# Audio tower on one core: gates of the power attention by a broadcast load, expert outputs added by DMA, a second attention in groups of three tiles, and its causal mask written into PSUM by TensorE

## The chip, the core and the metric

The kernel runs on one core of one Trainium2 chip. The metric is the device time of one launch in microseconds (us). Each engine (PE is the matrix engine, DVE the vector engine, ACT the scalar engine, POOL GpSimd, SP the engine that issues most loads) works through a queue of its own in order, and semaphores tie the queues together. The matrix engine has two clock levels, 1.2 and 2.4 GHz; the profile gives the granted clock as a share of full speed.

## The reference

64 sequences of 23 patches give 1472 tokens of 512 features. Five parts follow one another, each added to the running state h:

```python
h = tok(x)                      # layer norm, x @ W + b, layer norm
h = h + power_attention(ln(h))  # 8 heads, 2 query groups each, width 128
h = h + moe(ln(h))              # 16 experts, 4 per token, and a shared one
h = h + attention(ln(h))        # 16 query heads, 4 key heads, width 32
h = h + bitlinear_ffn(ln(h))    # ternary weights, width 2048
```

Of these, three places are touched.

```python
logG = jnp.cumsum(log_g, axis=1)                 # power attention
gate = logG[:, :, :, None] - logG[:, :, None, :]
a = jnp.where(causal, qk ** 2 * jnp.exp(gate), 0.0)
...
acc + cw[:, None] * _swiglu_ffn(x, wg, wu, wd)   # sum over a token's experts
...
scores = jnp.where(causal[None, None], scores, -jnp.inf)   # attention
A = jax.nn.softmax(scores, axis=-1)
```

## The kernel before

The tokens lie in 12 tiles of 128 rows, or, where whole sequences matter, in 16 blocks of 92 tokens (4 sequences), of which 4 make a chunk of 368 columns. fp32 products are made of three fp16 matmuls (high by high, low by high, high by low; L852 to L854), and a "low" part is made by `split_lo` on DVE (L1295).

**Power attention.** A hardware loop over 8 heads, in it 4 chunks. Per chunk PE projects q, k and v from the transposed state (`nT_hi`, `nT_lo`) with the unit's weights `wa_hi`, `wa_lo`, makes scores (L950), multiplies by v (L967), turns the result `yn` (L983) and applies the output weights. DVE accumulates the outputs (L1432). The decay gate of a chunk wants, in each of 92 rows, the cumulative logs of all 368 columns. They are made by an fp32 matmul of `ones` by `Dg` (L935), where `Dg` is the log gates spread over a triangle by DVE (L1447); ACT copies the result out of PSUM (`gt`, L635), and DVE subtracts the row's own sum and adds the mask. At the last chunk of a head the next head's weights are made: ACT writes `wa_hi` (L550) and DVE `wa_lo` (L1295, `unit_a_lo`), next to pieces of the experts' weights `we_sp` (`expert_hi`, `expert_lo`) that are prepared during the heads. Ahead of the loop stand the gate's logits, their logs `lg`, and one cumulative matmul by the triangle `tri` (L904).

**Experts.** 61 routed tiles leave weighted outputs `yt` in a table in DRAM, `yslot`. Then, on POOL's queue, `collect(k)` issues four indirect gathers per tile k of 128 tokens (L484, 48 in all) into a ring of three tiles' buffers, and DVE adds the four rows of `wide` to h (`returned`, L1698 to L1701). For the layer norm ahead of the second attention DVE makes sums, POOL the inverse square root of the variance (`root`, L446; eight tiles, then four), and ACT normalises (L560). ACT copies the turned tile into fp16 (L565), DVE makes the low part.

**Second attention.** The work is in 4 chunks c of 16 sequences. `project(c, j)` makes five blocks of q and k and one of v on PE; per block DVE shuffles halves (L1743), POOL multiplies by cosine and sine (L516, L517) and DVE adds (L1753, L1754). `scores(c)` is 64 fp32 matmuls of 32 x 23 (L1177, 128 recorded) into four banks of PSUM. `centred(c)` on DVE adds the mask (L1761, 128 x 1472), takes the maximum (L1764) and subtracts it (L1765); ACT takes the exponent; `weights(c)` sums (L1771) and divides (L1777); PE turns the weights (`turn`, L1186) and multiplies by V (`weighted`, L1199); ACT and DVE make high and low parts of the result (`y_high`, `y_low`, L1784). The order is written out by hand, in each engine's own function: PE does scores(c), all projections of c+1, turn(c), weighted(c). At the end the output weights and the ternary feed-forward follow.

## Time and profile before

| | us |
|---|---|
| three runs | 1563.63, 1563.95, 1555.3 |
| median | 1563.63 |
| profiled execution, its own time | 1547.85 |
| its span | 1545.9 |

| stage, us from the span's start | |
|---|---|
| tokens to state, layer norms | 0 to 145 |
| eight heads of the power attention | 151 to 700 |
| routing | 715 to 800 |
| experts, 61 routed tiles and the shared one | 800 to 1145 |
| gathers of the expert outputs | 1124.3 to 1196 |
| second attention | 1196.5 to 1340.6 |
| its output weights, then the feed-forward | 1340.6 to the end |

Over the whole span PE is busy 85%, DVE 61%, ACT 42%, POOL 18%. A share over the span mixes stages with different limits, so the profile is read stage by stage: first which engine is busy there, then what the others wait for.

### The profile page before, as it was taken

What the parts mean: (1) busy time and instruction counts of PE and PEld (TensorE: products, weight loads), DVE (VectorE), ACT (ScalarE), POOL (GpSimd) and SP (SyncE); (2) the same over time, 40 slices, a digit from 0 to 9 for tenths busy, and PEclk for the clock granted to TensorE, in tenths of its full rate; (3) what the DMA queues carried; (4) which work ended last, traced back from release to release, by engine and by line L of the source; (5) the groups of instructions that cost most, each with busy time, mean ns of one, the idle gap of its engine ahead of it and who ended that gap; (6) DMA issues with size and microseconds to landing.
All of it is one profiled execution on the core that took longest, in us unless ns stands there. A gap on an engine that the chain in (4) does not pass through costs nothing.

```text
span 1545.9 us, 30851 instructions
## 1 busy us (share of the span) xinstructions
PE 1316.9 (85%) x10735; PEld 837.6 (54%) x10736; DVE 937.2 (61%) x1940; ACT 644.0 (42%) x1098; POOL 283.0 (18%) x342
## 2 busy tenths in 40 slices
PE   6887999999999999996759999999950788668997
PEld 3445767677776777774424444444520566424443
DVE  5775456556665555658663555554376455588886
ACT  3445434444444444542314444444420433126664
POOL 2443000000000000000012233233276334020000
PEclk9986999999999999996779999999985778689999
DMA  5222142423334342421315767874265000000000
GB/s 177 69 102 69 56 170 116 163 109 135 133 132 170 136 163 82 163 83 75 132 62 181 258 240 256 283 241 162 91 193 168 2 2 3 1 1 8 21 20 31
DMA packets 40254, 179.87 MB, mean 116 GB/s; under 512 B 8512, under 2 KB 9024, under 8 KB 32384
## 3 DMA queue, kind: packets, MB, share of 16 engines
q0 software_dynamic: 18208, 95.41, 17.4%
q1 hardware_dynamic: 18528, 71.03, 13.0%
q10 hardware_dynamic: 3456, 12.58, 2.4%
q8 instruction: 41, 0.67, 0.2%
q14 instruction: 21, 0.17, 0.0%
HBM read 131.32 MB, written 47.69 MB: 116 GB/s over the span
## 4 chain that ended last, share of the span: by engine, by line
PE 56%; DVE 18%; issue 13%; POOL 6%; ACT 5%; DVEq 1%; DMA 1%; ACTq 0%; POOLq 0%; SPq 0%
PE ps L852 14%; PE ps L853 13%; PE ps L854 13%; POOL wide L484 3%; PE ps L967 3%; PE ps L950 3%; PE ps L1177 2%; DVE ff L1870 2%; DVE amf L1877 1%; PE ps L935 1%; PE ps L983 1%; DVE wa_lo L1295 1%; POOL rt_out L446 1%; PE ps L1046 1%; PE ps L1248 1%
## 5 line engine op out<-in xcount | busy, mean ns | idle before, releaser
L852 PE MATMUL ps<-nT_hi,wa_hi 128*128 128x368 f16 x448 | 146.4, 327 | 15.9 <-DVE wa_lo L1295 15.9
L853 PE MATMUL ps<-nT_lo,wa_hi 128*128 128x368 f16 x448 | 146.0, 326 | 0.0
L854 PE MATMUL ps<-nT_hi,wa_lo 128*128 128x368 f16 x448 | 145.6, 325 | 0.0
L476 POOL DMA_INDIRECT xg<-xrow,idx x61 | 61.1, 1001 | 277.1 <-PE ps L1046 101.7
L1629 DVE SCALAR_TENSOR_TENSOR nrm<-ps,xg,nrm 128x256 f32<-128x256 f32 x61 | 29.5, 484 | 133.5 <-ACT nrm L694 107.6
L852 PE MATMUL ps<-wa_hi,nT_hi 128*92 128x128 f16 (+1 forms) x560 | 108.8, 238 | 0.0
L853 PE MATMUL ps<-wa_lo,nT_hi 128*92 128x128 f16 (+1 forms) x560 | 107.6, 236 | 0.0
L854 PE MATMUL ps<-wa_hi,nT_lo 128*92 128x128 f16 (+1 forms) x560 | 107.6, 236 | 0.0
L852 PE MATMUL ps<-wide,xT 128*128 x244 | 93.4, 383 | 12.3 <-issue 6.3
L663 ACT ACTIVATE yT_hi<-ps 128x368 f16<-128x368 f32 x64 | 27.2, 474 | 164.0 <-PE ps L983 164.0
L471 POOL DMA_DIRECT2D wsp<-we_sp x16 | 8.6, 537 | 468.7 <-DVE we_sp L1295 468.7
L1432 DVE SCALAR_TENSOR_TENSOR wide<-ps,wide 128x368 f32<-128x368 f32 x128 | 69.1, 540 | 41.0 <-PE ps L854 41.0
L853 PE MATMUL ps<-wide,xT 128*128 x244 | 93.2, 382 | 0.0
L854 PE MATMUL ps<-wide,xT 128*128 x244 | 93.0, 381 | 0.0
L1248 PE MATMUL ps<-qw,qT 128*128 128x512 bf16 x384 | 89.1, 387 | 2.7 <-DVE ff L1870 2.6
L852 PE MATMUL ps<-yT_hi,wb_hi 128*128 128x368 f16 x256 | 82.6, 323 | 1.2 <-DVE yT_lo L1479 1.2
L853 PE MATMUL ps<-yT_lo,wb_hi 128*128 128x368 f16 x256 | 82.6, 323 | 0.0
L854 PE MATMUL ps<-yT_hi,wb_lo 128*128 128x368 f16 x256 | 82.6, 323 | 0.0
L622 ACT ACTIVATE qk<-ps 128x368 f32<-128x368 f32 x96 | 45.2, 478 | 89.1 <-PE ps L854 89.0
L1457 DVE TENSOR_TENSOR a<-sq,E 92x368 f32<-92x368 f32 x64 | 31.7, 534 | 82.3 <-ACT sq L651 82.3
L852 PEld LDWEIGHTS ps<-wa_hi,nT_hi 128*92 128x92 f16 (+1 forms) x560 | 67.4, 120 | 22.3 <-ACT qk L622 17.2
L685 ACT ACTIVATE xT<-ps 128x1024 f16<-128x1024 f16 x61 | 62.3, 1024 | 28.9 <-PE ps L1046 21.2
(307 smaller groups left out, 3403.9 us busy)
## 6 DMA issues: line engine op xcount, KB each, us to landing
we_st<-in_we POOLq DMA_DIRECT2D x16, 1536.0 KB, 6.9
wsp<-we_sp POOLq DMA_DIRECT2D x16, 1536.0 KB, 5.4
wide<-wsp SPq DMA_DIRECT2D x16, 1536.0 KB, 7.4
yslot<-yt POOLq DMA_DIRECT2D x61, 256.0 KB, 4.3
wq_st<-in_ffq SPq DMA_DIRECT2D x24, 512.0 KB, 4.5
wq_st<-in_ffq ACTq DMA_DIRECT2D x24, 512.0 KB, 3.9
wide<-in_wa SPq DMA_DIRECT2D x10, 1024.0 KB, 4.8
xt<-in_x SPq DMA_DIRECT2D x12, 512.0 KB, 3.5
```

The lines of the kernel that those rows point to most:

```text
L476: pool.indirect_dma_start(Q["xg"][:, g % 4, :].bitcast(U32), None, xrow, bass.IndirectOffsetOnAxis(ap=idx[:, g:g + 1], axis=0)).then_inc(x ...
L484: pool.indirect_dma_start(h1[:, 4 * (k % 3) + j, :], None, yslot, bass.IndirectOffsetOnAxis(ap=slot[:, k, j:j + 1], axis=0)).then_inc(xg_i ...
L622: nc.scalar.activation(B["qk"][:, j, :], ps[:, (5 * c + j) % 2, 0:CW], ACT.Copy, scale=1.0 / WS).then_inc(b_ev, 1)
L685: nc.scalar.activation(Q["xT"][:, p].rearrange("p a b -> p (a b)"), ps[:, p, :].bitcast(F16), ACT.Copy).then_inc(m_xe, 1)
L852: nc.tensor.matmul(dst, lhs[0], rhs[0], start=start, stop=False)
L853: nc.tensor.matmul(dst, lhs[0], rhs[1], start=False, stop=False)
L854: return nc.tensor.matmul(dst, lhs[1], rhs[0], start=False, stop=stop)
L950: ins = nc.tensor.matmul(ps[0:AT, 2 + j, a * REP * AT:(a + 1) * REP * AT], B["qk"][:, 2, tok], B["qk"][:, 0:2, tok], start=True, stop=True)
L967: ins = nc.tensor.matmul(ps[0:AT, 4 + 2 * j + a, r * (DH + 1):(r + 1) * (DH + 1)], B["a"][0:AT, j, a, r, :], B["v1"][0:AT, 2 * j + a, :], ...
L1248: ins = nc.tensor.matmul(ps[:, 2 * (f % 2) + q, :], Gm["qT"][:, b, ds(k * P, P)], qw[:, q, b * FF + f * 512:b * FF + (f + 1) * 512], start ...
L1432: V.scalar_tensor_tensor(acc, ps[:, 6 + blk % 2, 0:CW], 1.0 / (WS * AS), acc, ALU.mult, ALU.add).then_inc(b_acc, 1)
L1457: V.tensor_tensor(B["a"][0:AT, j], B["sq"][0:AT, j], B["E"][0:AT, 2 * j:2 * j + 2].unsqueeze(2).broadcast_to([AT, 2, REP, AT]), ALU.mult). ...
```

## The change

Four things are done.

1. The gates' cumulative logs for the columns no longer come from a matmul per chunk. One more matmul ahead of the heads gives them transposed (128 rows: 16 blocks by 8 heads); they are copied to SBUF, stored to DRAM (`lgd`), and once per head a broadcast load on SP's queue writes the head's row of 1472 values into 92 partitions (`gr`). The first of DVE's two passes reads `gr` instead of ACT's copy. The gate's logits move to another bank of PSUM, and two projections of the first head stand ahead of the cumulative matmuls. `unit_a_hi` and `unit_a_lo` are issued ahead of `expert_hi` and `expert_lo(., 0)` at a head's last chunk.
2. The gathers add into h themselves. `share(k, j)` waits until the transfer before it to the same tile has landed. DVE's adds are gone. The tiles come in four groups of three, with layer norm and root per group, and the gathers of the later groups stand between POOL's cosines.
3. The second attention's order is written anew: `turn(c - 1)` and `weighted(c - 1)` are done during chunk c, layer-norm tiles of the next group lie between projections, and most of the multiplications by the sine go from POOL to DVE.
4. The mask is written into PSUM by a bf16 matmul of identity by mask per bank (4 per chunk) ahead of the scores, which then accumulate on it; DVE's mask pass is gone, and its maximum and its subtraction read PSUM.

The diff, cut to its core:

```diff
+            sp.wait_ge(g_lg, 2)
+            sp.dma_start(lgd.rearrange("h (a p) -> (h a) p", p=AT), B["lgt"][:, :]).then_inc(init_out, 16)
+            sp.wait_ge(init_out, 32)
+            sp.dma_start(B["gr"][0:AT], lgd[0:1, :].broadcast_to([AT, T])).then_inc(gr_in, 16)
...
+                sp.wait_ge(b_gr, i + 1)
+                sp.dma_start(B["gr"][0:AT], lgd[ds(i + 1, 1), :].broadcast_to([AT, T])).then_inc(gr_in, 16)
...
-            def collect(k):
-                for j in range(TOPK):
-                    pool.indirect_dma_start(h1[:, 4 * (k % 3) + j, :], None, yslot,
-                                            bass.IndirectOffsetOnAxis(ap=slot[:, k, j:j + 1], axis=0)).then_inc(xg_in[k % 3], 16)
-
-            pool.wait_ge(zero_out, 16)
+            def share(k, j):
+
+                if j or k >= 6:
+                    pool.wait_ge(sh_in[k % 6], SHARES[k % 6] + 64 * (k // 6) + 16 * j)
+                pool.indirect_dma_start(h[:, k, :], None, yslot, bass.IndirectOffsetOnAxis(ap=slot[:, k, j:j + 1], axis=0),
+                                        compute_op=ALU.add).then_inc(sh_in[k % 6], 16)
+
+            def shares(g, j):
+                for k in range(GT * g, GT * g + GT):
+                    share(k, j)
...
-            for k in range(NT):
-                if k >= 3:
-                    pool.wait_ge(c_h, ready(NT + k - 3))
-                collect(k)
-
-            for n, x in enumerate((slice(0, EARLY), slice(EARLY, NT))):
-                root(rc_ask, 2 + n, rt_in[:, x], rt_out[:, x], rc_done)
+
+            def turned_root(g):
+                x = slice(GT * g, GT * g + GT)
+                root(rc_ask, 2 + g, rt_in[:, x], rt_out[:, x], rc_done)
...
+                if c and j < 4:
+                    nc.gpsimd.tensor_tensor(Fm["qs"][:, j, :], Fm["qs"][:, j, :], sinT[:], ALU.mult).then_inc(f_cos, 1)
+
+            for j in range(TOPK):
+                shares(0, j)
+                shares(1, j)
+            pool.wait_ge(m_y, VT)
+            shares(2, 0)
+            turned_root(0)
+            nc.gpsimd.memset(Fm["qp"][:, :, :, SL:], 0.0).then_inc(f_pad, 1)
+            shares(3, 0)
+            turned_root(1)
+            cosine(0, 0)
+            shares(2, 1)
+            cosine(0, 1)
+            cosine(0, 2)
+            shares(2, 2)
+            cosine(0, 3)
+            cosine(0, 4)
+            shares(2, 3)
+            pool.wait_ge(wa_lo, UNITS + 1)
+            nc.gpsimd.memset(st_a[:], 0.0).then_inc(f_pad, 1)
+            shares(3, 1)
+            for j in range(5):
+                cosine(1, j)
+            shares(3, 2)
+            turned_root(2)
+            shares(3, 3)
+            turned_root(3)
+            for c in range(2, CH):
...
-                    pe.wait_ge(b_ev, free(5 * g + 3))
-                    pe.wait_ge(b_D, g + 1)
-                    nc.tensor.matmul(ps[0:AT, (5 * c + 3) % 2, 0:CW], ones[0:AT, 0:AT], B["Dg"][0:AT].rearrange("p a b -> p (a b)"),
-                                     start=True, stop=True).then_inc(b_pj, 1)
...
+            pe.wait_ge(g_lg, 1)
+            nc.tensor.matmul(ps[0:AT, 7, 0:16 * HEADS], tri[0:AT, :], B["lg"][0:AT].rearrange("p a b -> p (a b)"),
+                             start=True, stop=True)
+            nc.tensor.matmul(ps[:, 6, 0:AT], B["lg"][0:AT].rearrange("p a b -> p (a b)"), tri[0:AT, :],
+                             start=True, stop=True).then_inc(g_cum, 1)
...
+                for g in range(G4):
+                    nc.tensor.matmul(ps[:, 2 + g, 0:CW], identb[:], maskb[:], start=True, stop=False)
                 for s in range(16):
                     for g in range(G4):
                         d = slice(HD * g, HD * (g + 1))
                         ins = nc.tensor.matmul(ps[:, 2 + g, s * SL:(s + 1) * SL], Fm["qp"][d, s].rearrange("p j t -> p (j t)"),
-                                               Fm["kr"][d, s * SL:(s + 1) * SL], start=True, stop=True)
+                                               Fm["kr"][d, s * SL:(s + 1) * SL], start=False, stop=s == 15)
...
+                if c + 1 < CH:
+                    pe.wait_ge(f_sb, c + 2)
+                else:
+                    pe.wait_ge(f_lo, 4 * c)
...
+            def row_turn_l1(k):
+                ln_turn(2 * NT + k, k % 2, k % 2)
+
+            for k in range(GT):
+                row_turn_l1(k)
+            pe.wait_ge(wa_lo, UNITS)
             pe.wait_ge(wb_lo, UNITS)
-            for j in range(3, 6):
-                project(0, j)
+            project(0, 0)
+            project(0, 1)
             for c in range(CH):
+                k = GT * (c + 1)
+                for j in range(2, 6):
+                    project(c, j)
+                    if c % 2 == 0 and j < 5:
+                        row_turn_l1(k + j - 2)
+                if c:
+                    turn(c - 1)
+                if c == 0:
+                    project(c + 1, 0)
+                    project(c + 1, 1)
                 scores(c)
-                if c + 1 < CH:
-                    for j in range(6):
-                        project(c + 1, j)
-                turn(c)
-                weighted(c)
+                if c == 1:
+                    weighted(c - 1)
+                    for j in range(GT):
+                        row_turn_l1(k + j)
+                if 0 < c < CH - 1:
+                    project(c + 1, 0)
+                    project(c + 1, 1)
+                if c > 1:
+                    weighted(c - 1)
+            turn(CH - 1)
+            weighted(CH - 1)
...
-                    V.tensor_tensor(B["Dg"][0:AT], B["lgh"][0:AT, 4 * c:4 * c + 4].unsqueeze(2).broadcast_to([AT, 4, AT]),
-                                    tri[0:AT].unsqueeze(1).broadcast_to([AT, 4, AT]), ALU.mult).then_inc(b_D, 1)
-                    dve.wait_ge(b_ev, ready(5 * g + 3))
-                    order(V.tensor_tensor(B["gt"][0:AT], B["gt"][0:AT],
+                    if c == 0:
+                        dve.wait_ge(gr_in, 16 * (i + 1))
+                        dve.sem_inc(passed, 1)
+                    order(V.tensor_tensor(B["gt"][0:AT], B["gr"][0:AT, c * CW:(c + 1) * CW].rearrange("p (a t) -> p a t", a=4),
...
+                    if c == CH - 1:
+                        unit_a_lo(i + 1)
                     if c % 2:
                         expert_lo(2 * i + c // 2, 0)
-                    if c == CH - 1:
-                        unit_a_lo(i + 1)
...
-            def returned(k):
-                dve.wait_ge(xg_in[k % 3], SLOTS_IN[k % 3] + 64 * (k // 3 + 1))
-                dve.sem_inc(passed, 1)
-                y = [h1[:, 4 * (k % 3) + j, :] for j in range(TOPK)]
-                V.tensor_tensor(y[0], y[0], y[1], ALU.add)
-                order(V.tensor_tensor(y[2], y[2], y[3], ALU.add))
-                order(V.tensor_tensor(row(k), row(k), y[0], ALU.add))
-                V.tensor_tensor(row(k), row(k), y[2], ALU.add).then_inc(c_h, 1)
...
-                order(V.tensor_tensor(S.rearrange("p (g h) s -> p g h s", g=G4),
-                                      ps[:, 2:6, 0:CW].rearrange("p g (h s) -> p g h s", s=SL),
-                                      mask1[:].unsqueeze(1).unsqueeze(1).broadcast_to([P, G4, 16, SL]), ALU.add))
-                order(V.tensor_reduce(Fm["mx"][:], S, AX.X, ALU.max))
-                V.tensor_tensor(S, S, Fm["mx"][:].unsqueeze(2).broadcast_to([P, 64, SL]), ALU.subtract).then_inc(f_sb, 1)
+                src = ps[:, 2:6, 0:CW].rearrange("p g (h s) -> p g h s", s=SL)
+                mx = Fm["mx"][:].rearrange("p (g h) -> p g h", g=G4)
+                order(V.tensor_reduce(mx, src, AX.X, ALU.max))
+                V.tensor_tensor(S.rearrange("p (g h) s -> p g h s", g=G4), src, mx.unsqueeze(3).broadcast_to([P, G4, 16, SL]),
+                                ALU.subtract).then_inc(f_sb, 1)
...
+            def low(k):
+                ln_low(2 * NT + k, k, k % 2)
+
+            for k in range(GT):
+                low(k)
+            group_shift(1)
             for c in range(CH):
+                k = GT * (c + 1)
+                rotate(c, 0)
+                rotate(c, 1)
+                if c:
+                    weights(c - 1)
+                for j in range(2, 5):
+                    if c % 2 == 0:
+                        low(k + j - 2)
+                    rotate(c, j)
+                rotated(c)
+                if c == 0:
+                    dve.wait_ge(wa_hi, UNITS + 1)
+                    split_lo(wo[1][:].rearrange("p a b -> p (a b)"), st_a[:], wo[0][:].rearrange("p a b -> p (a b)"), wa_lo)
+                if c == 1:
+                    group_stats(2)
+                    group_shift(2)
                 centred(c)
-                if c + 1 < CH:
-                    for j in range(2):
-                        rotate(c + 1, j)
-                weights(c)
-                if c + 1 < CH:
-                    for j in range(2, 5):
-                        rotate(c + 1, j)
-                    rotated(c + 1)
-                y_low(c)
+                if c:
+                    y_low(c - 1)
+                if c == 1:
+                    for j in range(GT):
+                        low(k + j)
+                    group_stats(3)
+                    group_shift(3)
+            weights(CH - 1)
+            y_low(CH - 1)
```

How rows move on three engines. First POOL before the change, from the last keeps of expert outputs (`yslot<-yt`) over the gathers to the first cosines; `rt_out` is the inverse square root, `qraw` and `qs` are a projected block and its shuffled copy.

```order
L480 DMA yslot<-yt 128x512 x6
L484 DMA wide<-yslot,slot 128x512 x48
L446 TENSOR_TENSOR rt_out<-rt_in,neg_half 128x8
L446 TENSOR_TENSOR rt_out<-rt_in,neg_half 128x4
L516 TENSOR_TENSOR qraw<-qraw,cosT 128x368
L517 TENSOR_TENSOR qs<-qs,sinT 128x368
```

The same place after the change.

```order
L501 DMA yslot<-yt 128x512 x6
L507 DMA h<-yslot,slot 128x512 x27
L467 TENSOR_TENSOR rt_out<-rt_in,neg_half 128x3
L550 MEMSET qp 128x64x9
L507 DMA h<-yslot,slot 128x512 x3
L467 TENSOR_TENSOR rt_out<-rt_in,neg_half 128x3
L540 TENSOR_TENSOR qraw<-qraw,cosT 128x368
L507 DMA h<-yslot,slot 128x512 x3
L540 TENSOR_TENSOR qraw<-qraw,cosT 128x368 x2
L507 DMA h<-yslot,slot 128x512 x3
L540 TENSOR_TENSOR qraw<-qraw,cosT 128x368 x2
L507 DMA h<-yslot,slot 128x512 x3
```

Of the gathers 27 now stand ahead of the first root, and 21 more come later, in groups of three between roots, fills and cosines.

DVE at the last chunk of a head, before: the accumulation of the outputs, then the two splits, then the normalising factor `rn` of `yn`.

```order
L1432 SCALAR_TENSOR_TENSOR wide<-ps,wide 128x368
L1437 REGISTER_ALU
L1295 SCALAR_TENSOR_TENSOR we_sp<-we_st,we_sp 128x1024
L1298 REGISTER_ALU
L1295 SCALAR_TENSOR_TENSOR wa_lo<-wide,wa_hi 128x2048
L1471 TENSOR_SCALAR rn<-ps 92x4
```

And after.

```order
L1538 SCALAR_TENSOR_TENSOR wide<-ps,wide 128x368
L1403 REGISTER_ALU
L1400 SCALAR_TENSOR_TENSOR wa_lo<-wide,wa_hi 128x2048
L1543 REGISTER_ALU
L1400 SCALAR_TENSOR_TENSOR we_sp<-we_st,we_sp 128x1024
L1578 TENSOR_SCALAR rn<-ps 92x4
```

The split of `wa_lo` now stands ahead of that of `we_sp`; what follows both is as it was.

PE in the second attention, before: V's projection, turn, weighting, the next chunk's scores, its next projections.

```order
L1161 MATMUL ps<-wb_lo,nT_hi 32x128 x4
L1161 MATMUL ps<-wb_hi,nT_lo 32x128 x4
L1186 MATMUL ps<-ident,wide 128x128 x16
L1199 MATMUL ps<-wide,V 32x92 x64
L1177 MATMUL ps<-kr,qp 128x23 x64
L852 MATMUL ps<-nT_hi,wa_hi 128x368
L853 MATMUL ps<-nT_lo,wa_hi 128x368
```

And after, at the chunk c = 1.

```order
L1238 MATMUL ps<-wb_hi,nT_lo 32x128 x4
L1270 MATMUL ps<-ident,wide 128x128 x16
L1256 MATMUL ps<-maskb,identb 128x368 x4
L1260 MATMUL ps<-kr,qp 128x23 x64
L1287 MATMUL ps<-wide,V 32x92 x64
L925 MATMUL ps<-ident,nrm 128x128 x12
L930 MATMUL ps<-nT_hi,wa_hi 128x368
L931 MATMUL ps<-nT_lo,wa_hi 128x368
```

The turn of the chunk before is now ahead of the scores, the weighting behind them, and three tiles of layer norm are turned (`nrm`, L925) before the next projection; the four mask matmuls are the row ahead of the scores.

## Rows read from the trace of the kernel before

The engines' columns of the first group are PE, PEld, DVE, ACT and POOL in this order.

**Rows 1.** Busy time: us, engines' busy time (instructions), PE clock, DMA share, GB/s.

```profile
287.30:355.70 68.40, 66.12 (x570) 49.79 (x569) 40.55 (x80) 30.00 (x51) 2.15 (x4) 1.00 0.37 138
...
1145.00:1196.00 51.00, 0.03 (x1) 0.00 (x0) 35.54 (x60) 1.18 (x2) 37.29 (x33) 0.53 0.65 194
```

**Rows 2.** Timeline, ACT: start, us, engine, line, operation, [idle before <-releaser].

```profile
1196.52 1.52 ACT L560 ACTIVATE nrm<-h,nb,rt_out 128x512 f32<-128x512 f32 x2 [50.34 <-DVE nb L1327]
```

**Rows 3.** Timeline, PE in the second attention.

```profile
1228.94 7.04 PE L1177 MATMUL ps<-kr,qp 32*128 32x23 f32 x128 [6.87 <-DVE qp L1754]
...
1259.54 7.04 PE L1177 MATMUL ps<-kr,qp 32*128 32x23 f32 x128 [3.82 <-DVE nT_lo L1784]
...
1317.19 7.04 PE L1177 MATMUL ps<-kr,qp 32*128 32x23 f32 x128 [3.80 <-DVE nT_lo L1784]
...
1338.73 1.83 PE L1199 MATMUL ps<-wide,V 32*32 32x92 f32 x128
```

**Rows 4.** Groups of instructions: form, count, busy us, mean ns, idle before.

```profile
L935 PE MATMUL ps<-Dg,ones 92*92 92x368 f32 x64 | 25.7, 483 | 0.0
```

**Rows 5.** Timeline, PE around one gate matmul in a head.

```profile
272.85 0.32 PE L854 MATMUL ps<-nT_hi,wa_lo 128*128 128x368 f16 x1
273.01 0.78 PE L935 MATMUL ps<-Dg,ones 92*92 92x368 f32 x2
273.74 0.26 PE L852 MATMUL ps<-wa_hi,nT_hi 128*92 128x128 f16 x1
```

**Rows 6.** DMA issues: tile<-source, queue, count, KB each, median us to landing.

```profile
wide<-in_wb SPq DMA_DIRECT2D x10, 512.0 KB, 3.5
...
tb<-in_tb SPq DMA_DIRECT2D x1, 256.0 KB, 9.2
```

**Rows 7.** Timeline, PE in the first head.

```profile
151.30 0.73 PE L904 MATMUL ps<-lg,tri 92*92 92x128 f32 x2 [6.13 <-DVE lg L1418]
...
165.52 1.93 PE L967 MATMUL ps<-v,a 92*92 92x129 f32 x16
```

**Rows 8.** Timeline, PE at the boundary of two heads.

```profile
285.68 0.33 PE L852 MATMUL ps<-nT_hi,wa_hi 128*128 128x368 f16 x1 [2.28 <-DVE wa_lo L1295]
...
287.56 0.80 PE L983 MATMUL ps<-ident,yn 92*128 92x92 f32 x8
```

**Rows 9.** Timeline, DVE at the same boundary.

```profile
282.13 1.22 DVE L1295 SCALAR_TENSOR_TENSOR we_sp<-we_st,we_sp 128x1024 f16<-128x1024 f32 x1
283.26 2.29 DVE L1295 SCALAR_TENSOR_TENSOR wa_lo<-wide,wa_hi 128x2048 f16<-128x2048 f32 x1
...
286.85 0.69 DVE L1473 TENSOR_TENSOR yn<-ps,rn 92x512 f32<-92x512 f32 x1
```

**Rows 10.** Timeline, POOL: the first, third and last of 48 gathers.

```profile
1124.34 1.00 POOL L484 DMA_INDIRECT wide<-yslot,slot  x1 [2.02 <-DMA yslot<-yt]
...
1126.93 0.95 POOL L484 DMA_INDIRECT wide<-yslot,slot  x1 [0.30 <-issue]
...
1189.23 1.02 POOL L484 DMA_INDIRECT wide<-yslot,slot  x1 [0.30 <-issue]
```

**Rows 11.** Instructions of the line of the gathers: their landing times.

```profile
DMA to landing us min/median/max: 3.3/3.7/7.3
```

**Rows 12.** Timeline, DVE: the softmax of chunk 0.

```profile
1236.05 1.69 DVE L1761 TENSOR_TENSOR wide<-ps,mask 128x1472 f32<-128x1472 f32 x1 [7.16 <-PE ps L1177]
...
1239.50 1.69 DVE L1765 TENSOR_TENSOR wide<-wide,mx 128x1472 f32<-128x1472 f32 x1
...
1245.25 1.69 DVE L1771 TENSOR_REDUCE rd<-wide 128x64 f32<-128x1472 f32 x1 [1.99 <-ACT wide L747]
...
1247.56 1.69 DVE L1777 TENSOR_TENSOR wide<-wide,rd 128x1472 f32<-128x1472 f32 x1
```

**Rows 13.** Groups of instructions: POOL's multiplication by the cosine.

```profile
L516 POOL TENSOR_TENSOR qraw<-qraw,cosT 128x368 f32<-128x368 f32 x20 | 19.4, 968 | 71.8 <-DVE qs L1743 71.8
```

**Rows 14.** Busy time, PE alone, scores(0): us, busy, clock, DMA share, GB/s.

```profile
1228.90:1236.00 7.10, 7.05 (x129) 0.50 0.01 2
```

More of the change, by code:

```diff
@@ L390, in _ @@
                 unit_b(i + 1)
+                sp.wait_ge(b_gr, i + 1)
+                sp.dma_start(B["gr"][0:AT], lgd[ds(i + 1, 1), :].broadcast_to([AT, T])).then_inc(gr_in, 16)
+            sp.wait_ge(q_abs, 3 * HEADS - 2)
+            for m in range(3):
+                sp.dma_start(wq_st[:, m, :], t["ffq"][m, HEADS - 1]).then_inc(q_in, 16)
+            sp.wait_ge(wa_lo, HEADS)
+            unit_a(HEADS)
+            sp.wait_ge(wb_lo, HEADS)
+            unit_b(HEADS)
             for k in range(NT):
@@ L771, in _, with normed @@
[L771 to L784 removed]
+            def normed(k):
+                if k % GT == 0:
+                    act.wait_ge(ln_sh, 3 + k // GT)
+                ln_norm(2, k, k % 2)
@@ new lines, in high @@
+            def high(k):
+                ln_high(2 * NT + k, k, k % 2)
+            normed(0)
+            normed(1)
+            high(0)
+            normed(2)
+            high(1)
+            high(2)
+            moved(0, 0)
+            moved(0, 1)
+            for c in range(CH):
+                k = GT * (c + 1)
+                if c % 2 == 0:
+                    normed(k)
+                    normed(k + 1)
+                moved(c, 2)
+                if c % 2 == 0:
+                    high(k)
+                    normed(k + 2)
+                moved(c, 3)
+                if c % 2 == 0:
+                    high(k + 1)
+                moved(c, 4)
+                if c % 2 == 0:
+                    high(k + 2)
+                moved(c, 5)
+                if c == 0:
+                    act.wait_ge(wa_in, 16 * (UNITS + 1))
+                    nc.scalar.activation(wo[0][:].rearrange("p a b -> p (a b)"), st_a[:], ACT.Copy, scale=WS).then_inc(wa_hi, 1)
+                else:
+                    weights_turned(c - 1)
+                if c == 1:
+                    normed(k)
+                    normed(k + 1)
+                    exponential(c)
+                    y_high(c - 1)
+                    high(k)
+                    normed(k + 2)
+                    high(k + 1)
+                    high(k + 2)
+                    moved(c + 1, 0)
+                    moved(c + 1, 1)
+                else:
+                    if c + 1 < CH:
+                        moved(c + 1, 0)
+                        moved(c + 1, 1)
+                    exponential(c)
+                    if c:
+                        y_high(c - 1)
@@ L786, in f_square @@
+            weights_turned(CH - 1)
+            y_high(CH - 1)
             def f_square(k, p, half):
@@ L1236, in q_turn @@
                 ins.then_inc(w_tr, 1)
-            pipeline(pe, NT, [(0, out_rows)])
+            for k in range(NT):
+                out_rows(k, k % 2, k // 2)
             def gate_up(k, fs):
@@ L1421, in _ @@
             dve.wait_ge(g_cum, 1)
+            V.tensor_copy(B["lgt"][:], ps[:, 6, 0:AT]).then_inc(g_lg, 1)
             order(V.tensor_copy(B["LG"][0:AT].rearrange("p a b -> p (a b)"), ps[0:AT, 7, 0:128]))
```

157 lines of the change are left out of this document (64 added, 93 removed).

## The prediction

> **What bounds the kernel.** I read, in this order, busy time by stretch, the costliest lines, the timelines of the places that the diff touches, and the landing times of transfers. In the steady heads PE is the limit: of the 68.40 us of one head it is busy 66.12, at full clock, while DVE has 40.55 and ACT 30.00 [rows 1]. What leaves PE there leaves the end; what leaves DVE or ACT does not. Before the second attention it is the reverse: from 1145 to 1196 us PE does nothing, and POOL is busy 37.29 of 51.00 with issuing the gathers of the expert outputs [rows 1]. ACT idles 50.34 us and begins the second attention at 1196.52 [rows 2]. That stage runs to 1340.56, 144.0 us, and no engine bounds it: the rows show PE waiting for the rotated operands, for the weights, for the low half of V's operand [rows 3]. It is a chain of hand-overs.
>
> **Heads: the gate matmul.** Each of 32 chunks (8 heads, 4 chunks) had one fp32 matmul of ones by Dg, recorded in two halves, 64 of 0.483 us [rows 4]. What counts is its slot: the row before it starts at 272.85 and gives way after 0.16 (the pace of its neighbours), the row after starts at 273.74 [rows 5], so 0.73 us. 32 x 0.73 = **-23.4 us**, all on the path. Its ACT eviction and the DVE product go too, at nothing, since both engines wait for PE. In its place stand one small matmul ahead of the heads and one broadcast load per head, 529 KB, on SP's queue. Chunk 0 of a head waits for it; it is issued when the head before has read its last quarter. The nearest row is a 512 KB load, 3.5 us [rows 6]; the slowest near it is 9.2 us for 256 KB, at the start. A head's first gate is wanted about ten us after its first matmul, and DMA was at 0.37 of its capacity in a head [rows 1], so loads 2 to 8 hide.
>
> **First head.** PE idled 6.13 us ahead of the cumulative matmul, for DVE's logs [rows 7]. Two projections now stand ahead of it and fill that idle time. The first AV came at 165.52; its gates now need lgt, a store, the load of 3.5 us and the passes behind it, and I get about 161.5: 4.0 us, 0.7 of which is the first Dg slot already counted, so **-3.3** (bounds -4.7, load hidden, and +1, load at 9.2). The load has 92 rows on both sides. The Trainium skill, page "DMA: Bandwidth & Descriptors", section "Why a DMA increments its semaphore by 16 and not by 1", says that a transfer uses the largest number of engines up to 16 that divides both outer sizes: 4 here. By its 27 GiB/s an engine the load lands, as an estimate, after 6.7 us and the sum gives 3.2 us less; no row of this profile shows a load of 92 partitions.
>
> **Boundary of heads.** PE waits 2.28 us for wa_lo [rows 8], seven times. DVE splits an expert's weights first (1.22 us), then wa_lo, then makes yn [rows 9]. The change swaps the two, so wa_lo lands 1.2 us sooner. But PE's matmul L983 wants yn, whose last piece is made from 286.85 to 287.54, and L983 starts at 287.56 [rows 8, 9]: the same DVE passes stand ahead of yn in either order. The wait is renamed from wa_lo to yn; I take 0.25 each, **-1.7** (bounds 0 and -8.5, where all 1.2 us come through). Heads together: -28.4.
>
> **Start of the second attention.** POOL issued 48 gathers, from 1124.34 to 1189.23: 1.38 us each [rows 10]. Then came the root of eight tiles, and ACT at 1196.52. Now the groups are of three tiles, and 27 issues stand ahead of the first root: 1124.34 + 27 x 1.38 = 1161.6; root and shift 1.4; ACT starts at 1163.0, **-33.5**. The four DVE adds per tile that followed the landings are gone: the transfer adds. Each tile takes four of them in a row, and POOL waits for one to land before it issues the next to that tile. A round over six tiles is 6 x 1.38 = 8.3 us, over the longest landing of a plain gather, 7.3 (median 3.7) [rows 11], so at plain prices the wait costs nothing. The accumulating form is nowhere in this profile. Bounds: bare pace 1.25 an issue (0.95 and 0.30 [rows 10]) gives -37; every landing at twice the maximum, 14.6 us a round, puts the last round at 1124.3 + 43.8 = 1168, its landings at up to 1185 and the start at 1188, -8.5. Bus time of a plain gather: 0.65 of 51 us at 194 GB/s, 256 KB each, is 37.7 gathers, 0.88 us each [rows 1]; twice that, 1.76, is above the pace of 1.38: the last share of the first group, 21st in line, lands at 1124.3 + 37 + 3.7 = 1165, and the start is about 3 later, -30.5. The Trainium skill, page "Collectives: The Full Stack", section "The bandwidth ceiling: the fold count and why AG ≠ RS ≠ AR", says just that: an adding transfer reads two sources and runs at half the rate. By it the sum gives 3 us less; no row here shows it.
>
> **Length of the second attention.** The 21 other gathers, 29 us of POOL, now lie within it, between cosines. I went through the new order leg by leg. (a) Start to scores(0): 32.4 before (1228.94 - 1196.52), now 26: three tiles' layer norm instead of eight, but 9 gathers between the cosines (range 22 to 32.4). (b) scores(0) to scores(1): 23.6 before (1259.54 - 1235.98), now 19: centring 3.4 (two passes of 1.69; the mask pass is gone, and its row shows that reading PSUM costs no more), exponent about 4.1 (from 1241.19 to 1245.25, where its sum starts), weights 4.0 (1245.25 to 1249.25) [rows 12], five cosines of 0.97 [rows 13], rotation 2.2. (c) scores(1) to scores(2), all on PE or waited for by it: centring 3.4, weighting 1.8, y_high 1.6, three layer-norm tiles 4 and their turns 2, six projections 14.3 (72 matmuls at 0.2, between 0.16 at full clock [rows 5] and twice that), turn 3, hence 30. (d) scores(2) to scores(3): the same without layer norm, turns and y_high, 22.5. (e) Four score blocks, 4 x (7.04 + 0.62) = 30.6; the 0.62 is four mask matmuls of 368 columns, 0.16 us apart at full clock like the head's [rows 5]. (f) Tail: 16.3 before (1340.56 less 1317.19 + 7.04 [rows 3]), now 16.6: one DVE pass of 1.7 less, y(2) ahead of the last weights 2.3 more. Sum 144.7 against 144.0, +1. The mask by itself is thus worth -1.7 x 4 + 0.6 x 4 = -4. Clock: scores(0) came after 6.87 us of idle PE and ran at a granted 0.50, so at 1.2 GHz [rows 3, 14]. Now scores(0) and scores(2) follow busy PE; I take -4 (between 0, no change, and -14, all four at the full 2.4 GHz: half of 28). Stage net **-3** (range -14 to +10: leg (a) +6.4, the others +4).
>
> **Sum.** -28.4 - 33.5 - 3.0 = -64.9. The profiled execution took 1547.85 (span 1545.9), which gives 1483. It stood 15.8 under the median of its runs, 1563.63, with one run at 1555.3. Against the median: **1499 us**. Under 1% of 1563.63, 15.6 us, this kernel can hardly be told from no change.
>
> **The rivals.**
> - *Landings set the pace* (chance 0.15). POOL waits in every round; the share of bus time, 0.65 already [rows 1], speaks for it, the 8.3 us round against 3.7 speaks against. At 14.6 a round, 25 us of the gain are gone: 1524.
> - *The queues of the new second attention collide* (0.12). PE, DVE and POOL are in order, and weights(c-1) now stands between the rotations of c; a late gather in POOL holds the cosines, these the scores. At 6 us for each of legs (a) to (d) less overlap, 20 are lost: 1519.
> - *Clock stays high* (0.15). PE is fed through all four score blocks, -10 more than I take: 1489. Against it, PE idle before scores, 6.87 and 3.8 us [rows 3], is not all filled.
> - *Slower than before* (0.03). The adding gather is bound by its own rate. The gain of the heads, 28.4, stays, so ACT would have to start 31.4 us later than 1196.5, and the tail of gathers for later groups end past the cosines: from 3.7 us a gather ((1302 - 1124.3)/48), four times the 0.88 of bus time, the kernel is slower. For it: only that nothing here shows the form.
> - *My sum* has 0.55. The -23.4 of the gate matmul is as safe as a row can make it, which is why the signs hardly mix.
>
> The range: the low end is the forecast with the high clock and the whole boundary wait (-10, -6.8) and something of the first head, 1476 to 1479, and 3 for the runs' spread; the high end is the first rival and 8 more. I take 1474 to 1533. Faster by over 1%: all but the slow rival and half of a stack of the first two, 0.93; within 1% 0.04; slower 0.03.
>
> **What would show it.** In the changed profile: a head of about 65.2 us (68.40 less 4 x 0.73 and 0.25) with PE busy for 63, no matmul on Dg, and no wait for the broadcast load after the first head; PE's wait at a boundary still near 2 us, but now for yn; ACT's first row of the second layer norm at 1196.5 - 28.4 - 33.5, about 1135; gathers issued 1.38 apart with no wait for a landing; the stage from there about 141 us; two DVE passes of 1.7 instead of three between scores and exponent; granted clock over 0.5 in scores(0). A round of gathers over 10 us, a wait of POOL for landings, or scores 25 us apart in leg (b) would make the sum wrong, and a head of still over 67.5 us would refute the first step.

## The result, and the profile after

The changed kernel took 1511.69 us (median of 4 runs, 1510.18 to 1513.29) against 1560.72 of the kernel before: a ratio of 0.9689 (95% interval 0.9655 to 0.9724), 49 us less. When both were measured again, on one chip, they took 1509.55 and 1551.43, 0.9743 (0.9720 to 0.9767), 42 us less. The forecast was 1499, 65 us less; the direction and the range (1474 to 1533) held, the size was a third too large. The two profiled executions differ by less still: spans 1545.9 and 1510.1, so 35.8. The kernel before has a wide spread: its 27 runs lie between 1547.0 and 1564.0, and its profiled one, 1547.85, is among its fastest. The changed kernel's 9 lie between 1508.9 and 1513.6. Why, is read from experiment e5 below; the account of steps goes by the two traces.

First, busy time of a head, in the columns of [rows 1].

```profile
284.23:349.38 65.15, 63.58 (x560) 48.94 (x561) 38.21 (x75) 28.22 (x47) 2.16 (x4) 1.00 0.41 153
```

A head takes 65.15 instead of 68.40, PE is busy 63.58 of it: the period held to 0.1 us and PE's busy time to 0.6 (65.2 and 63 were forecast). The timeline of PE, first head, first boundary, and then the scores of the second attention, to the first matmul of its output weights ([rows 7], [rows 8] and [rows 3] are the same places before).

```profile
167.20 3.72 PE L1037 MATMUL ps<-v,a 92*92 92x129 f32 x16 [5.36 <-DVE a L1564]
...
219.07 0.33 PE L930 MATMUL ps<-nT_hi,wa_hi 128*128 128x368 f16 x1 [1.11 <-DVE wa_lo L1400]
222.11 0.54 PE L1053 MATMUL ps<-ident,yn 92*128 92x92 f32 x4 [0.46 <-DVE yn L1580]
...
1187.09 0.80 PE L1256 MATMUL ps<-maskb,identb 128*128 128x368 bf16 x4 [2.51 <-DVE qp L1851]
1187.81 7.03 PE L1260 MATMUL ps<-kr,qp 32*128 32x23 f32 x128
...
1212.86 1.41 PE L1256 MATMUL ps<-maskb,identb 128*128 128x368 bf16 x4 [5.18 <-DVE qp L1851]
1214.19 7.04 PE L1260 MATMUL ps<-kr,qp 32*128 32x23 f32 x128
...
1252.21 3.77 PE L1260 MATMUL ps<-kr,qp 32*128 32x23 f32 x128
...
1278.56 1.41 PE L1256 MATMUL ps<-maskb,identb 128*128 128x368 bf16 x4 [3.60 <-DVE qp L1851]
1279.89 7.04 PE L1260 MATMUL ps<-kr,qp 32*128 32x23 f32 x128
...
1304.94 0.39 PE L930 MATMUL ps<-wo_hi,nT_hi 128*128 128x512 f16 x1
```

The boundary's wait is split, 1.11 for wa_lo and 0.46 for yn. The first AV product (the gated scores `a` by v) starts at 167.20, later than before (165.52), after 5.36 us of idle PE, and takes 3.72 instead of 1.93. Why it is late, DVE's timeline says: the first row that reads the broadcast load.

```profile
164.47 0.54 DVE L1555 TENSOR_TENSOR gt<-gr,LGh 92x368 f32<-92x368 f32 x1 [10.06 <-DMA gr<-lgd]
```

SP issued that load at 155.27, so it took 9.2 us. DVE waited for no other of the eight loads. Now POOL: first, second and 27th gather, and the first root ([rows 10]).

```profile
1103.99 1.66 POOL L507 DMA_INDIRECT h<-yslot,slot  x1 [2.02 <-DMA yslot<-yt]
1105.96 1.57 POOL L507 DMA_INDIRECT h<-yslot,slot  x1 [0.30 <-issue]
...
1154.49 1.55 POOL L507 DMA_INDIRECT h<-yslot,slot  x1 [0.31 <-issue]
1155.48 1.47 POOL L467 TENSOR_TENSOR rt_out<-rt_in,neg_half 128x3 f32<-128x3 f32 x1
```

An adding gather holds POOL for 1.55 us where a plain one held it for 0.95, and the next starts 1.85 later (1.94 on average, 50.50 / 26, with two that took longer). No wait of POOL for a landing costs time: one of the 48 gathers is released by a landing, and it starts after the same 0.31 as its neighbours. ACT begins the second attention at 1157.19 ([rows 2]):

```profile
1157.19 1.52 ACT L607 ACTIVATE nrm<-h,nb,rt_out 128x512 f32<-128x512 f32 x2 [32.19 <-DVE nb L1432]
```

| step | forecast | in the traces |
|---|---|---|
| up to the first gather (1124.34 to 1103.99) | -28.4 | -20.4 |
| first gather to ACT's start (72.18 to 53.20) | -33.5 | -19.0 |
| length of the second attention (144.0 to 147.7) | -3 | +3.7 |
| behind it | 0 | -0.2 |
| sum | -64.9 | -35.8 |

### The profile page after: what moved, and what is told of

It reads as the page before. It is cut to its first block, busy times and chain, and to the rows that moved or that the text cites. A ratio compares the mean times of both kernels' runs of the same rounds, so it can differ in the third digit from the quotient of the medians.

```text
span 1510.1 us, 30384 instructions
## 1 busy us (share of the span) xinstructions
PE 1302.2 (86%) x10676; PEld 833.5 (55%) x10690; DVE 889.8 (59%) x1862; ACT 630.0 (42%) x1066; POOL 308.1 (20%) x336
## 4 chain that ended last, share of the span: by engine, by line
PE 55%; DVE 18%; issue 13%; POOL 6%; ACT 4%; DMA 2%; DVEq 1%; ACTq 0%; POOLq 0%; SPq 0%
PE ps L930 13%; PE ps L932 13%; PE ps L931 13%; POOL h L507 3%; PE ps L1037 3%; PE ps L1020 3%; PE ps L1260 2%; DVE ff L1980 2%; DVE amf L1987 1%; PE ps L1353 1%; PE ps L1053 1%; POOL rt_out L467 1%; PE ps L1121 1%; PE ps L1371 1%; DMA xg<-xrow,idx 1%
## 5 line engine op out<-in xcount | busy, mean ns | idle before, releaser
L930 PE MATMUL ps<-nT_hi,wa_hi 128*128 128x368 f16 x448 | 147.7, 330 | 11.9 <-DVE wa_lo L1400 8.1
L507 POOL DMA_INDIRECT h<-yslot,slot x48 | 79.7, 1661 | 15.4 <-issue 13.1
```

The source lines that it names most:

```text
L507: pool.indirect_dma_start(h[:, k, :], None, yslot, bass.IndirectOffsetOnAxis(ap=slot[:, k, j:j + 1], axis=0), compute_op=ALU.add).then_inc ...
L930: nc.tensor.matmul(dst, lhs[0], rhs[0], start=start, stop=False)
```

## The experiments

All are edits of the changed kernel. They ran on three chips, each beside runs of the kernel before, whose medians there were 1556.9 (e1, e2, e4, e6), 1552.0 (e3, e5, e7, e8) and 1551.4 (e9 and the last three). A total that is 1 or 2 us off that of the changed kernel (1511.7, again 1509.6) therefore settles nothing by itself; the traces do.

Terms: a "leg" is the time from one block of scores to the next, or from ACT's start to the first, or from the last to the output weights; the "tail" is that last leg; the "stage" is the whole second attention, from ACT's start to the first matmul of the output weights.

**e2 and e3: why the first broadcast load took 9.2 us.**

```diff
# e2, likewise at the load in the loop
-            sp.dma_start(B["gr"][0:AT], lgd[0:1, :].broadcast_to([AT, T])).then_inc(gr_in, 16)
+            sp.dma_start(B["gr"][0:96], lgd[0:1, :].broadcast_to([96, T])).then_inc(gr_in, 16)
# e3
             sp.dma_start(B["gr"][0:AT], lgd[0:1, :].broadcast_to([AT, T])).then_inc(gr_in, 16)
+            sp.wait_ge(gr_in, 16)
```

> The changed kernel with the broadcast load of the gate's row written to 96 partitions instead of 92. In the changed kernel the first of these loads took 9.2 us, and the first AV product of head 0 stood idle 5.36 us for it, starting at 167.20. Theory A, 92 rows are spread over few DMA engines (the Trainium skill, DMA: Bandwidth & Descriptors, Why a DMA increments its semaphore by 16 and not by 1: 4 for 92, 16 for 96): it lands after 3 to 4.5 us, the product starts at about 162 to 163, total 4 to 6 us less, 1506 to 1508. Theory B, it is slowed by the other loads then in flight (feed-forward weights, head weights, the expert weights): landing stays near 9 us, total 1512.

> The changed kernel, but SP issues nothing behind the first broadcast load of the gate's row until it has landed, so that three 512 KB feed-forward loads and the head's weights don't run beside it. Theory A, few DMA engines for 92 rows set its 9.2 us: it lands only 0 to 2 us sooner, total 1510 to 1512. Theory B, the loads beside it set it: it lands after 4 to 5 us, first AV product at 162 to 163, total 1506 to 1508.

e2: 1504.19. The load is issued at 155.12 and used at 159.33, 4.2 us, though it moves more bytes beside the same neighbours. e3: 1508.04; issued at 154.75, used at 161.49, 6.7 us with nothing beside it. How many engines carried it can be read from the DMA share while it ran alone:

```profile
156.00:161.00 5.00, 4.44 (x44) 3.42 (x41) 0.00 (x0) 0.59 (x1) 0.00 (x0) 1.00 0.26 102
```

The last two columns are DMA share and GB/s: 0.26 of 16 engines is 4.2, about the 4 of theory A in e2. The AV product of e2 on PE's timeline, and PE's clock in the 5 us from it (us, busy, clock, DMA share, GB/s):

```profile
162.06 1.97 PE L1037 MATMUL ps<-v,a 92*92 92x129 f32 x16 [1.18 <-DVE a L1564]
```

```profile
162.06:167.06 5.00, 5.00 (x41) 1.00 0.92 374
```

The same window of the changed kernel:

```profile
167.20:172.20 5.00, 5.00 (x21) 0.50 0.43 158
```

So theory A of e2 holds (few engines for 92 rows), with a share for the neighbours: of 9.2 us, 5.0 go with four more rows, 2.5 with the neighbours gone (between the two theories of e3). The estimate worked out in the prediction from the Trainium skill (DMA: Bandwidth & Descriptors, Why a DMA increments its semaphore by 16 and not by 1), 6.7 us for 4 engines, is what e3 measured; 4.7 of it are 541,696 bytes over four engines, and where its other 2.0 come from it does not say. The rest of the gain is the clock: after 5.36 us of idle PE the granted clock was 0.50, 1.2 GHz, for these 5 us; after 1.18 it was 1.00. From the start of AV to the first boundary it is 51.87 us in the changed kernel and 48.49 in e2, so e2's first boundary comes 8.5 sooner: 5.1 by AV's start, 3.4 by the clock. Its first gather, at 1096.78, is 7.2 sooner; the stretch from the last boundary to the gathers differs from that of the changed kernel by up to 2 us in most traces, and by 3.7 in e3's.

**e5: the swap at a head's end.** On ACT and DVE the expert's piece stands ahead of the next head's weights again:

```diff
# DVE; ACT's expert_hi and unit_a_hi likewise
-                    if c == CH - 1:
-                        unit_a_lo(i + 1)
                     if c % 2:
                         expert_lo(2 * i + c // 2, 0)
+                    if c == CH - 1:
+                        unit_a_lo(i + 1)
```

> The changed kernel with only the swap undone: at a head's last chunk the expert's piece is split ahead of the next head's weights, on ACT and DVE, as before. The changed kernel waits 1.11 for the weights and 0.46 for yn at each of 7 boundaries, the one before 2.28. Theory A (the swap is what took the 0.7 off): period of a head 65.16 grows to about 65.9, total 5 us more, 1516 to 1517. Theory B (the prediction's: yn sets it in either order): period within 0.3, total within 2 us of 1511.7.

1517.19, about 5.5 us over the changed kernel, as theory A has it, but not by its reason, a period of 65.9: the period is that of neither theory. PE waits 2.24 us for wa_lo at all seven boundaries, and from one to the next it is 67.06, 65.39, 67.06, 65.40, 65.39, 67.05 us. PE in the 5 us behind the first four:

```profile
218.90:223.90 5.00, 4.99 (x26) 0.66 0.58 210
285.95:290.95 5.00, 4.98 (x36) 1.00 0.59 210
351.35:356.35 5.00, 4.99 (x26) 0.66 0.59 210
418.40:423.40 5.00, 4.98 (x36) 1.00 0.59 210
```

Where the clock holds, the swap is worth 65.39 - 65.16 = 0.24 a boundary, the 0.25 of the prediction. Where it falls (219, 351, 549), the head takes 1.66 longer. Six periods give 6 x 0.24 + 3 x 1.66 = 6.4, which is what the last boundary of e5 is late. Behind the waits of 1.11 every period is 65.2 in all twelve other traces of the changed kernel and its edits. The kernel before has the same long wait, 2.28, and its profiled execution shows 1.00 behind all its boundaries and a period of 68.37 throughout. That other executions of it lost 1.66 at some of seven boundaries, up to 11.6 us, would explain most of its spread over 17 us, which does not come from the three chips alone (nine runs on one of them lie between 1547.0 and 1559.6): of 23 runs whose mean clock is known, those at 0.917 took 1547.0 to 1548.0, the one at 0.906 took 1559.6 (the correlation of time and clock is -0.69). This is argued from e5 and these numbers, not shown; no slower execution of the kernel before was profiled.

**e1 and e9: the adding gather.**

```diff
 # e1 and e9
-                ... axis=0),
-                                        compute_op=ALU.add).then_inc(sh_in[k % 6], 16)
+                ... axis=0)).then_inc(sh_in[k % 6], 16)
 # e9 too: no gather ahead of the last shared expert tile
+            pool.wait_ge(m_y, VT)
             for j in range(TOPK):
                 shares(0, j)
                 shares(1, j)
-            pool.wait_ge(m_y, VT)
```

> The changed kernel with its 48 gathers made plain: the adding form is taken off, target, order and waits stay. The output leaves the addition out (a gather overwrites the row). In the changed kernel an adding gather holds POOL for 1.54 us, 1.85 from one to the next, where a plain one held it 0.95. Theory A, the adding form is dearer to issue: back to about 1.25 to 1.38 a gather, landings back from 7.4 to about 4 us, DMA share while they run from 0.89 back to about 0.6, ACT starts the second attention 27 x 0.5 = 13 us sooner, total 1496 to 1500. Theory B, the price comes from the target (rows of h, in use by others) or from the waits for landings: pace stays 1.85, total stays at 1512.

> The plain gathers again (addition left out), but none issued before the last shared expert tile is done, so that PE's matmuls of that tile and the gathers no longer run at once. In the kernel with plain gathers PE stood for 8.43 and 6.60 us on issue while 24 of them ran, the last shared tile came 19 us late, and POOL waited 10.24 us for it. Theory A (the gathers in flight held up PE's instructions, and the plain form is cheaper to issue): no such stall, last shared tile near 1124, first gather about 1125, 27 gathers 1.26 apart, ACT starts about 36 us after the first gather (53.2 in the changed kernel), near 1161. Theory B (the stall is PE's own): it stays, and gathers start near 1144. Total 1512 to 1517 under A, 1530 under B.

e1: 1507.98. Theory A is right on the price (0.95 a gather, 1.26 from one to the next, the same target and order), and its total was missed. (The 7.4 us that its expectation gives for a landing are counted from the gather before; from the right one they are 5.5 to 5.8.) POOL's timeline after 24 gathers, and the waits of PE in that time:

```profile
1132.81 0.95 POOL L507 DMA_INDIRECT h<-yslot,slot  x1 [0.30 <-issue]
1144.01 2.76 POOL L507 DMA_INDIRECT h<-yslot,slot  x1 [10.24 <-DVE h L1742]
```

```profile
PE ps L929 <- issue: 8.4, 1, 8.4
PE ps L1137 <- issue: 6.6, 1, 6.6
```

PE, busy with the last shared expert tiles, stood 15 us with no wait that the profile shows, so `m_y`, the sign that the last of these tiles is done, came at 1143.7 instead of 1124.6. e9, which keeps the two apart, has no such stall: its last shared tile is done at 1128.2, it issues its first 27 gathers from 1129.04 to 1163.17, 1.31 apart, and ACT starts at 1165.27, 36.2 us after the first gather against 53.2. The stage behind it, with dearer gathers no longer between the cosines, takes 140.0 instead of 147.7 us; 2.1 of that are scores(0), which took 4.89 instead of 7.03. Its total is 1509.53, under the 1512 to 1517 expected: the plain form gives back the whole 25 us for which it was held. The transfers too are dearer: while the gathers run, busy share, bytes (columns of [rows 1]) of the changed kernel and of e9 are

```profile
1104.00:1155.00 51.00, 18.43 (x99) 8.60 (x97) 13.69 (x25) 9.14 (x16) 43.07 (x27) 0.72 0.89 149
```

```profile
1129.00:1165.20 36.20, 0.00 (x0) 0.00 (x0) 5.57 (x12) 0.00 (x0) 28.21 (x29) 0.51 0.73 218
```

or 0.89 x 51 / 29.0 = 1.57 us of all engines for 256 KB, against 0.73 x 36.2 / 30.1 = 0.88. That is the direction of the Trainium skill's rule (Collectives: The Full Stack, The bandwidth ceiling: the fold count and why AG ≠ RS ≠ AR), 1.8 times where it has 2; the page says it of the adding step of a ring collective, not of a gather. But 1.57 is under the 1.85 of POOL's issue: transport never set the pace.

**e4, e7, e8: the mask.** e4 takes the mask matmuls out and puts DVE's pass back. e7 and e8:

```diff
-                pe.wait_ge(f_rope, c + 1)
...
-                for g in range(G4):
-                    nc.tensor.matmul(ps[:, 2 + g, 0:CW], identb[:], maskb[:], start=True, stop=False)
+                for n in range(R):      # e7: 1; e8: (2, 3, 1, 3)[c]
+                    for g in range(G4):
+                        nc.tensor.matmul(ps[:, 2 + g, 0:CW], identb[:], maskb[:], start=True, stop=n < R - 1)
+                pe.wait_ge(f_rope, c + 1)
```

> The changed kernel with only the mask undone: no mask matmuls, DVE adds the mask out of PSUM before the maximum, as before. By the sum of the prediction the mask is worth 1.7 x 4 less 0.6 x 4: the second attention, 147.7 us in the changed kernel, gets 3 to 5 us longer, total 1515 to 1517. Rival: DVE's third pass lies in a leg whose end PE or POOL sets, and the mask matmuls are on PE's path at half clock (0.8 to 1.4 us a chunk), so that nothing is lost, total 1510 to 1513.

> The changed kernel with the four mask matmuls of a chunk ahead of PE's wait for the rotated operands, behind the wait for free banks. They take 0.8 to 1.4 us behind that wait now, at 3 of 4 chunks with PE idle ahead of it (2.51, 5.18, 3.60 us). Theory A: each of the three gives its 0.7 to 1.35 us, together 3.4, total 1508 to 1509. Rival: the banks are free too late, or PE's idle time only moves, total 1511 to 1512.

> As the kernel with the mask matmuls ahead of the wait, and these repeated (2, 3, 1, 3 times in the four chunks) so that PE has work in the 2.5 to 5.2 us in which it waited. Scores of chunks 0, 1 and 3 ran at 1.2 GHz, 7.04 us each, those of chunk 2, which followed busy PE, in 3.76. Theory A, the clock follows how busy PE was just before: the three score blocks fall to 3.8 to 5.5 us, total 4 to 9 us under the kernel without repeats, 1500 to 1505. Theory B: so few matmuls don't change the granted clock, and the repeats delay nothing, total 1508 to 1510, or cost 1 us a chunk where they outlast the wait.

e4: 1512.36, and the stage takes 149.45 us instead of 147.75: the mask by matmul is worth 1.7 us, not 4. Where: the tail is 2.0 longer without it, the leg from scores(1) to scores(2) 2.1, but that from scores(2) to scores(3) is 1.6 and the first 1.0 shorter, since the mask matmuls, 1.3 us and 0.7 us, have no cover there, while DVE's pass has cover in the one and does not occur in the other. The total fits the rival of its expectation, the stage lies between the two.

e7: 1507.49, stage 143.5, 4.2 less. Theory A holds: the legs that end at chunks 0, 1 and 3 are 1.1, 0.6 and 1.35 shorter, 3.0 for its 3.4. The leg to scores(2) is 0.5 longer, and 1.5 come from elsewhere: the last scores took 5.57 instead of 7.04, at a granted 0.65, and why is not shown.

e8: 1505.19, stage 142.1. PE's clock in e8's scores of chunks 0, 1 and 3:

```profile
1189.00:1193.90 4.90, 4.87 (x128) 0.74 0.57 72
1214.80:1221.40 6.60, 6.59 (x128) 0.54 0.78 115
1277.90:1283.10 5.20, 5.12 (x128) 0.71 0.02 3
```

In the changed kernel these three had 0.50, and chunk 2, behind busy PE, 1.00 in both. The repeats raise the clock in part: scores(0) took 4.95 instead of e7's 7.01. But the leg behind it is 2.1 longer than in e7, and PE waits at its end for qp, so that this gain is lost again. e8 is 1.5 us (stage) to 2.3 us (total) under e7.

**e6: POOL's queue.** Root 0 stands behind 26 gathers instead of 27, root 1 behind one more instead of three, later gathers where POOL was idle.

```diff
-            shares(2, 0)
+            share(6, 0)
+            share(7, 0)
             turned_root(0)
...
-            shares(3, 0)
+            share(8, 0)
             turned_root(1)
+            share(9, 0)
+            share(10, 0)
             cosine(0, 0)
...
```

> The changed kernel with POOL's queue in another order only: two instead of three gathers of group 2 ahead of root 0, one ahead of root 1, group 3's first ones behind it, its second round behind the second cosine of chunk 1 and its third around root 2. In the changed kernel DVE asked for root 0 at 1150.4 and POOL, in order behind gathers, made it at 1155.5; root 1 at 1162.5, asked at 1159.5. Theory A, POOL's queue sets the start: ACT begins 4.5 to 5 us sooner, scores(0) 5 to 8 us sooner, total 1503 to 1507. Theory B, PE's projections and the landings set it: the start moves but scores(0) under 2 us, total 1510 to 1512.

1510.22, and 1504.7 the span of the profiled execution, its fastest. Its first gather happened to be 3.0 us sooner, so times are counted from that: ACT's start 51.4 instead of 53.2 (one gather, not the 4.5 I had expected; two still stood ahead of the root), scores(0) 5.2 sooner, but scores(1) 2.7 and the output weights 2.4. The rest goes in the leg between, on PE:

```profile
1207.13 1.41 PE L1266 MATMUL ps<-maskb,identb 128*128 128x368 bf16 x4 [8.63 <-DVE qp L1861]
```

Half of theory A, though the total lies in the range of B: POOL's queue sets scores(0), and DVE's and POOL's rotation of chunk 1 sets scores(1).

**Together.** The changed kernel again, e2 with e8 (v1), and both with e6 (v2), on one chip.

> The changed kernel as it stands, to compare the two versions with on one chip. Its first runs had 1511.7 against 1560.7 of the kernel before, whose other runs since had medians of 1557 and 1552. If the change is worth what its trace against that of before shows (35.8), 0.975 to 0.977 of before; if what the first runs showed (49), 0.969.

> The changed kernel with the gate's load to 96 rows and the mask matmuls ahead of the wait and repeated (2, 3, 1, 3). Alone the two gave 1504.2 and 1505.2 against 1511.7. If they add, 1497 to 1499; if the clock's state, which both change, is shared between them, 1500 to 1504.

> As v1, with POOL's queue in the new order too. Alone it moved scores(0) 5.2 us nearer to the first gather, but the output weights only 2.4. If it adds to v1, 2 us less, 1495 to 1497; if the leg from scores(0) to scores(1) takes it all back, as v1.

1509.55, 1499.16 and 1496.12 against 1551.43: ratios 0.9743 (0.9720 to 0.9767), 0.9666 (0.9642 to 0.9691) and 0.9654 (0.9632 to 0.9677). v2 is 13.4 us under the changed kernel, in every run of five (1494.9 to 1499.7 against 1508.9 to 1513.6). v1 lies at the edge of "they add" (1497 to 1499). v1 to v2 is not told apart by the intervals; in the two traces v2 goes from the first gather to the output weights in 192.6 us instead of 195.8. Scores(0) of v2 ran at a granted 0.95, scores(1), behind 6.38 us of idle PE, at 0.50 again. The ratio of the changed kernel itself, 0.9743, is near the value that its trace gave (0.975 to 0.977) and its interval leaves out the other (0.969).

## Why the prediction was right in direction and too large in size

The medians flatter the sum. By the two traces, from which it was worked out, it is nearly twice too large (64.9 for 35.8). That the medians differ by 49 is luck: some 13 us of it come from the kernel before running slower in most executions than in its profiled one, and no term of the sum stands for that. Two of its own signs of being wrong came true: a round of six gathers took 11.1 us, over 10, and the granted clock in scores(0) was 0.50.

- **The gate matmul** (-23.4): right. Periods of 68.37 and, with the swap undone and the clock up, 65.39: 2.98 for four slots, 0.745 each for the 0.73 forecast.
- **The boundary** (-1.7): right in size where the clock holds (0.24 a boundary), though the wait was not renamed but split, 1.11 for wa_lo and 0.46 for yn. What the longer wait can cost in clock, 1.66 a time, was not in the sum. It may be part of why the medians differ by more than the traces (argued at e5).
- **The first head** (-3.3): failed. The step was "the nearest row is a 512 KB load, 3.5 us"; it took 9.2, the bound, and the AV product came 1.7 us later than before (167.2) instead of 4.0 sooner (161.5), 5.7 us for the load. The bound given for that case, +1, is a slip: by its own terms it is -3.3 + 5.7 = +2.4. The clock, which fell in the idle time, had no term; it took 1.8 for that product alone and 3.4 up to the first boundary. Together the first boundary came 8.2 us later than the sum had it, which is all that the heads miss (20.4 for 28.4). The page that spoke against the step had the size right for a load with nothing beside it (e3), and I had kept it out of the sum because no row showed a load of 92 partitions.
- **Start of the second attention** (-33.5): mechanism right, one term mis-sized, "27 x 1.38". An adding gather takes POOL 1.85 to 1.94. I had bounded its landing, 14.6 us a round, and its bus time, and not its issue, for which I took the plain row. 26 x (1.94 - 1.38) = 14.6 us, the whole of the missing 14.5. The first rival, landings, did not come about: landings, read from where DVE's sums of the first group start (1145.34, 1147.05 and 1149.19, for gathers issued at 1139.67, 1141.53 and 1143.38), were 5.5 to 5.8 us, under a round of 11.
- **Length of the stage** (-3): legs (c) and (d) were right (30.25 and 22.6 for 30 and 22.5), (b) was 18.0 for 19, (a) 29.9 for 26, the same dear gathers lying between its cosines (26.2 from ACT's start to the mask in e9), the tail 18.0 for 16.6 (its own terms, 16.3 - 1.7 + 2.3, give 16.9). The blocks of scores with their mask matmuls took 29.0 for 30.6, so that of the clock term, -4, only 1.6 came: scores(2), 3.77 us, ran at 2.4 GHz, the three others, 7.0 each, at 1.2. The mask was worth 1.7, not 4: a DVE pass was counted as on the path in all four chunks. PE's windows of scores(0) and scores(2):

```profile
1187.80:1194.80 7.00, 7.00 (x130) 0.50 0.65 102
1252.20:1256.00 3.80, 3.80 (x130) 1.00 0.02 4
```

- **Leg (b)** came out near its sum with a wrong part in it: the list of changes names most sine products as moved to DVE, but only 8 of 20 are, the five of chunk 0 and one of each later chunk. POOL has nine products of 0.97 in chunk 1, not five, and PE waits 5.18 for that rotation.
- Of the rivals, the colliding queues (1519) came true in a small part, the 3.9 us of leg (a). The high clock (1489) did not: the scores gained less from it than the sum had taken. Nor did slower than before.

## What to carry to other kernels

A new form of an instruction has a price in each queue that it passes: bound the engine that issues it as well as the transfer, and look where it is issued in a row. A load that an engine waits for is bounded by its row count too, and not only by the bytes of a load of other shape: here four more rows, 96 for 92, made it land in 4.2 us for 9.2. A wait of PE costs more than its length if the granted clock falls behind it, and work that depends on nothing belongs ahead of such a wait: the mask matmuls gave about 3 us by standing there.

## What the runs showed of the hardware that was not expected

- POOL is held 1.55 us by an adding indirect gather of 128 x 512 fp32 and 0.95 by a plain one. The root behind it is not slower, though its row has 1.47 us against 0.89 in e9: it starts at 1155.48, 0.56 before the gather's row ends, and the remaining 0.91 agree.
- 24 plain gathers at 1.26 us coincided with 15 us of PE standing still at matmuls that waited for nothing shown (e1); with adding ones, 1.85 apart, and with plain ones after the matmuls (e9), it did not happen. It did not happen in the kernel before either, where 17 plain gathers, into `wide` instead of h, ran beside the same matmuls from 1124.3 to 1146 and PE was busy 18.78 of 22.00 us. So plain gathers beside these matmuls are not enough for it. e1 has one trace, and what held PE is open.
- The clock fell behind three of seven waits of 2.24 us in one execution (e5), behind none of the seven of 2.28 in the kernel before, and behind none of 1.11.
- 92 rows loaded alone kept 0.26 of the 16 DMA engines busy (e3), and took 6.7 us; 96 rows took 4.2 beside other loads (e2).
